# Two row tiles per step in the first attention pass of a six-layer transformer kernel, and one PSUM bank for its side work

## The chip, the cores and the metric

The kernel runs on one core of one Trainium2 chip. The metric is the device time of one execution in microseconds; the time of a kernel is the median of several executions. A core has five engines with instruction streams of their own: TensorE (PE; its weight loads are shown apart, as PEld), VectorE (DVE), ScalarE (ACT), GpSimd (POOL) and SyncE (SP), which here issues the DMAs. Each stream is executed in its order, and streams wait for each other by semaphores. PSUM has eight banks of 128 x 512 float32; matmuls write there, and DVE and ACT read there.

## The reference

x is 4 sequences of 512 tokens of 256 channels. After a layer norm, six layers run, each of self attention, cross attention and a GELU network, and at the end a mixture of 8 experts with top-2 routing:

```python
NL, D, H, DFF = (6, 256, 16, 1024)
HD = D // H
...
def _attn(q, k, v, mask):
    scores = jnp.einsum('bqhd,bkhd->bhqk', q, k) / np.float32(np.sqrt(HD))
    scores = jnp.where(mask[:, None, None, :], jnp.float32(-jnp.inf), scores)
    w = jax.nn.softmax(scores, axis=-1)
    return jnp.einsum('bhqk,bkhd->bqhd', w, v)
...
for i in range(NL):
    xn = _adaln(x, noise_emb, n1_w[i], n1_b[i])
    q, k, v = jnp.split(xn @ qkv_w[i].T, 3, axis=-1)
    ...
    x = x + _attn(q, k, v, src_mask).reshape(B, L, D) @ so_w[i].T
    xn = _adaln(x, noise_emb, n2_w[i], n2_b[i])
    ...
    x = x + _attn(q, k, v, ctx_mask).reshape(B, L, D) @ co_w[i].T
    xn = _adaln(x, noise_emb, n3_w[i], n3_b[i])
    h = jax.nn.gelu(xn @ f1_w[i].T + f1_b[i], approximate=False)
    x = x + (h @ f2_w[i].T + f2_b[i])
```

(The quoted lines are slightly joined; q and k are rotated by position, and in cross attention k and v come from the context.) A head has only 16 channels, so the attention is 16 heads x 512 x 512 scores per sequence and attention.

## The kernel before

**Jobs and slots.** One attention of one sequence is a job: 8 jobs in a layer (4 self, 4 cross), 48 in all. The work is pipelined in slots. In slot k the engines run the first pass of job k, the second pass of job k-1, the end of job k-2 (normalise, output projection, and behind a cross job its feed-forward network), and the head of job k+1 (norm, query and key projections, splitting). Slots whose end has a feed-forward network are called long here, the others short; four short and four long ones alternate in a layer.

**The two passes.** Queries and keys are split into three bfloat16 parts (high, mid, low), and a score is the sum of six part products. The parts are written to DRAM (`bounce`) and loaded again as a stack of 6 x 16 = 96 rows for each head, so that one bfloat16 matmul with 96 to 99 rows gives all six products. The first pass (L719) computes for each head and each tile of 128 queries the scores (128 x 512) into one of three PSUM banks (`ps1`), and DVE takes the negative row maximum (L933). The maxima are turned (chunk "M"), copied by ACT, and a DMA puts them as two more rows into the query stack. The second pass (L694) computes the scores transposed and shifted by the maximum, in two banks (`ps2`), and ACT takes the exponential (L762) into `prob`. A matmul may fill a `ps2` bank only when the exponential two before it is done (`s_prob`). After every four exponentials four matmuls of 32 columns each (L707, four heads on four column tiles; float32, so that each is two instructions in the trace) add prob times v into `psv`.

**A unit.** A slot has 16 units. A unit on PE is four times (one first-pass matmul, one second-pass matmul), with the four-head product "pv" after the second of them. The order is written out in `slot` of the tensor block.

**Side chunks.** All else on PE is cut into chunks of one PSUM bank and put at one of 32 places (two in each unit) by `CHUNK_PLACES`, `FFN1_PLACES`, `FFN2_PLACES` and `SHIFT_PLACES`. Two banks `side` are used in turn: a chunk waits (`begin`) only for the reader of the chunk two before it. The chunks: T1 (transpose the attention output), T2, O (output projection), HT and LT (transposes of a normed tile; LT for the feed-forward network), HQ, HK, HV (query, key and value projection), M, F1 (feed-forward, first layer, 8 chunks in two bundles of four) and F2 (second layer, two chunks). T1, HQ, HK, O and F2 are read by DVE; HT, LT, T2, HV, M and F1 by ACT. F1's reader is the GELU itself (L834), with a table load ahead and behind.

**The splitting chain.** DVE multiplies HQ and HK with cosine and sine, POOL adds the terms (L557, L558), ACT rounds to the high part (L802), POOL takes the rest (L560), ACT the mid part (L806), POOL the low part (L562). When the low part is there, SP issues one write of all three parts (768 KB, once for the queries and once for the keys), waits for both, and issues the loads of the stacks: 12 DMAs of 128 KB and the mask row for heads 0 to 7 (`load_stack(j, 0)`), then the two shift rows of the job before, then as much for heads 8 to 15. The first pass of a job can begin when the stacks of heads 0 to 7 are there.

## Time and profile before

| what | value |
| --- | --- |
| time before, median of 3 runs | 4818.79 us (4811.88 to 4828.0) |
| span of the profiled execution | 4811.2 us |
| first first-pass matmul / last pv | 113 us / 4240 us |
| short slot, long slot | 67 to 68 us, 103 to 106 us |
| PE, DVE, ACT, POOL busy | 93%, 60%, 55%, 15% |
| mean granted TensorE clock | 0.963 of full speed |

The attention and feed-forward layers take 4127 us of the span; ahead of them lie 113 us of preparation, behind them 571 us with the last network and the experts. A PE record of a pipelined matmul lasts from its start to its modelled end, which is longer than the distance to the next one; so what a matmul costs is read from the distance of starts in the timeline, not from its mean.

### The profile page before, as it was taken

The page shows a single profiled execution, that of the slowest core. Times are in us where ns is not written, and L with a number is a line of the kernel's source. Part 1 is how long each engine was busy: PE and PEld are TensorE (multiplying, and loading weights), DVE is VectorE, ACT ScalarE, POOL GpSimd, SP SyncE. Part 2 cuts the span into 40 slices and gives each one's busy share as a digit, 9 for nine tenths or more (in the row PEclk, how much of TensorE's full clock was granted, in tenths as well). Part 3 has the DMA queues.
Part 4 walks back from the last instruction along what each step waited for, and adds up shares of the span by engine and source line. Part 5 has one row for each costly group of instructions (what it writes and reads, how often), then busy time and mean ns, then how long its engine had stood idle before and what let it go on. Part 6 is the DMA issues. An engine that isn't in the chain of part 4 may idle for free. (4 is left out here: it accounts for less than half of the span.)

```text
span 4811.2 us, 74161 instructions
## 1 busy us (share of the span) xinstructions
PE 4472.5 (93%) x21558; PEld 2219.7 (46%) x21558; DVE 2875.6 (60%) x5847; ACT 2636.0 (55%) x4666; POOL 734.4 (15%) x434
## 2 busy tenths in 40 slices
PE   3899999999999999999999999999999999968999
PEld 1244455433544444455434555344554334455666
DVE  3777656577666577655677555776566776322111
ACT  1466655566555566555566555666555665621221
POOL 3221111112121121111112111211111121000000
PEclk7899999999999999999999999999999999988999
DMA  5444422344322434232444223343223442010000
GB/s 146 75 98 78 74 48 46 69 89 78 61 42 52 82 72 89 48 59 41 86 89 80 41 41 54 88 81 74 46 49 68 89 80 50 1 36 9 18 18 26
DMA packets 165264, 297.17 MB, mean 62 GB/s; under 512 B 26352, under 2 KB 131840, under 8 KB 146432
## 3 DMA queue, kind: packets, MB, share of 16 engines
q1 hardware_dynamic: 164864, 292.23, 31.5%
q8 instruction: 202, 3.31, 0.3%
q14 instruction: 198, 1.62, 0.1%
HBM read 212.18 MB, written 77.59 MB: 60 GB/s over the span
## 5 line engine op out<-in xcount | busy, mean ns | idle before, releaser
L933 DVE TENSOR_REDUCE negmax<-ps 128x1 f32<-128x512 f32 x3072 | 1981.1, 684 | 754.5 <-PE ps L719 734.6
L762 ACT ACTIVATE prob<-ps 128x512 f32<-128x512 f32 x3072 | 1718.0, 595 | 1148.7 <-PE ps L694 1115.2
L719 PE MATMUL ps<-kstack,qstack 97*128 97x512 bf16 x3072 | 1200.6, 392 | 105.6 <-DMA kstack<-maskrow 56.3
L694 PE MATMUL ps<-qstack,kstack 99*128 99x512 bf16 x3072 | 1192.9, 389 | 84.8 <-ACT prob L762 65.5
L707 PE MATMUL psv<-prob,v 128*32 128x512 f32 x6144 | 832.8, 614 | 0.7 <-ACT prob L762 0.7
L719 PEld LDWEIGHTS ps<-kstack,qstack 97*128 97x128 bf16 x3072 | 300.6, 98 | 997.3 <-DVE negmax L933 599.0
L694 PEld LDWEIGHTS ps<-qstack,kstack 99*128 99x128 bf16 x3072 | 301.8, 98 | 646.9 <-ACT prob L762 454.8
L557 POOL TENSOR_TENSOR rot<-ropep 128x512 f32<-128x512 f32 x96 | 122.0, 1270 | 2624.2 <-DVE ropep L965 2593.3
L971 DVE TENSOR_TENSOR x<-x,side 128x512 f32<-128x512 f32 x144 | 99.0, 688 | 475.3 <-PE side L614 475.3
L673 PE MATMUL side<-anat,wf 128*128 128x256 f32 x1536 | 343.6, 382 | 0.9 <-ACT anat L792 0.9
L614 PE MATMUL side<-wf,hT 128*128 128x256 f32 x1536 | 339.9, 379 | 1.9 <-issue 1.9
L614 PEld LDWEIGHTS side<-wf,hT 128*128 128x128 f32 x1536 | 292.0, 190 | 46.8 <-issue 2.7
L673 PEld LDWEIGHTS side<-anat,wf 128*128 128x128 f32 x1536 | 290.4, 191 | 45.0 <-issue 5.5
L1336 DVE SCALAR_TENSOR_TENSOR x<-eps,we,x 128x256 f32<-128x256 f32 x128 | 56.1, 480 | 389.1 <-PE eps L1201 389.1
L1238 ACT ACTIVATE hg<-eps,b 128x512 f32<-128x512 f32 x128 | 88.0, 687 | 363.5 <-PE eps L1189 363.5
L562 POOL TENSOR_TENSOR parts<-rot,parts 128x1024 bf16<-128x1024 f32 x96 | 204.1, 2126 | 324.0 <-ACT parts L806 324.0
L560 POOL TENSOR_TENSOR rot<-rot,parts 128x1024 f32<-128x1024 f32 x96 | 204.6, 2132 | 273.0 <-ACT parts L802 273.0
L707 PEld LDWEIGHTS psv<-prob,v 128*32 128x32 f32 x6144 | 121.5, 108 | 263.5 <-issue 188.8
L834 ACT ACTIVATE hT<-side,f1b 128x256 f32<-128x256 f32 x384 | 160.9, 470 | 131.2 <-PE side L673 130.6
L1189 PE MATMUL eps<-zT,w 128*128 128x512 f32 x512 | 227.8, 598 | 0.8 <-DVE x L1317 0.8
L1201 PE MATMUL eps<-w,hg 128*128 128x256 f32 x1024 | 226.4, 379 | 0.0
L1201 PEld LDWEIGHTS eps<-w,hg 128*128 128x128 f32 x1024 | 194.4, 190 | 40.5 <-issue 9.6
(140 smaller groups left out, 3789.6 us busy)
## 6 DMA issues: line engine op xcount, KB each, us to landing
bounce<-parts SPq DMA_DIRECT2D x96, 768.0 KB, 3.7
qstack<-bounce SPq DMA_DIRECT2D x576, 128.0 KB
kstack<-bounce SPq DMA_DIRECT2D x576, 128.0 KB
ctxT<-in_ctxT SPq DMA_DIRECT2D x24, 512.0 KB, 5.5
nw<-in_nwT SPq DMA_DIRECT2D x18, 512.0 KB, 11.3
w<-in_w SPq DMA_DIRECT2D x16, 512.0 KB, 4.4
wself<-in_wself SPq DMA_DIRECT2D x24, 256.0 KB, 5.1
wcross<-in_wcross SPq DMA_DIRECT2D x24, 256.0 KB, 4.2
```

The lines of the kernel that those rows point to most:

```text
L560: nc.gpsimd.tensor_tensor(rot[:, :, :], rot[:, :, :], parts[:, 0, :, :], ALU.subtract).then_inc(s_r1, 1)
L562: nc.gpsimd.tensor_tensor(parts[:, 2, :, :], rot[:, :, :], parts[:, 1, :, :], ALU.subtract).then_inc(s_low, 1)
L614: mm = nc.tensor.matmul(bank[:, i * D:(i + 1) * D], act_T[:, k, t * P:(t + 1) * P], w[:, k, :], start=(k == 0), stop=(k == nk - 1))
L673: mm = nc.tensor.matmul(bank[:, i * D:(i + 1) * D], wf1[:, kk, f * P:(f + 1) * P], nT[:, kk, th * (S // 2):(th + 1) * (S // 2)], start=(kk ...
L694: nc.tensor.matmul(ps2[:, slot_of(j, n, RING2), :], kk[:, h, kt * P:(kt + 1) * P], q[:, h, :], start=True, stop=True).then_inc(s_p2full, 1)
L707: mm = nc.tensor.matmul(psv[32 * i:32 * i + 32, 0, :], v[j % B][:, kt, (HD + 1) * h:(HD + 1) * h + 32], prob[:, 4 * (u % 2) + i, :], start ...
L719: nc.tensor.matmul(ps1[:, slot_of(j, n, RING1), :], q[0:SHIFT_ROW, h, t * P:(t + 1) * P], kk[0:SHIFT_ROW, h, :], start=True, stop=True).th ...
L762: nc.scalar.activation(prob[:, 4 * (u % 2) + i, :], ps2[:, slot_of(j, n, RING2), :], ACT.Exp, scale=HD ** -0.5).then_inc(s_prob, 1)
L834: ins = nc.scalar.activation(hT[:, f, :], bank[:, i * D:(i + 1) * D], ACT.Gelu, bias=f1b[:, f:f + 1])
L933: nc.vector.tensor_reduce(negmax[:, h // 8, t, h % 8:h % 8 + 1], ps1[:, slot_of(j, n, RING1), :], AX, ALU.max, negate=True).then_inc(s_p1f ...
L1189: mm = nc.tensor.matmul(ps[:, f, :], w1[:, i, k, f * P:(f + 1) * P], zT[:, k, c * S:(c + 1) * S], start=(k == 0), stop=(k == KD - 1))
L1201: mm = nc.tensor.matmul(ps[:, 4 + 2 * (n % 2) + m, q * D:(q + 1) * D], hg[:, n % 2, f, t * P:(t + 1) * P], w2[:, i, f, :], start=(f == 0), ...
```

## The change

- The heads are taken in pairs, one of heads 0 to 7 with one of heads 8 to 15. Of each stack, three part products (48 rows) and a mask row lie in one half of the 128 partitions, and the other three in the other half, the halves swapped for heads 8 to 15. The first pass uses only the first three products (high x high, high x mid, mid x high), 49 rows, so the two heads of a pair stand in rows 0 to 48 and 64 to 112, and their two matmuls go to two row tiles and two PSUM banks. One `tensor_reduce` then gives both heads' maxima (128 x 2 from 128 x 1024). The second pass uses all rows from 0 to 113.
- `ps1` has four banks (two pairs), and `side` one in place of two: each chunk now waits for the reader of the chunk before it. All places are set anew, with tables for short and for long slots.
- A unit on PE is now: two second-pass matmuls, a chunk, four first-pass matmuls (two pairs), pv, two second-pass matmuls, a chunk.
- F1 is read by DVE, which adds the bias, and one GELU over 2048 elements (in place) takes each half; the F1 chunks lie at eight places in a row, and F2 is cut into four chunks.
- Each part is written to DRAM as soon as it is there, once for each product it is part of (12 writes of 256 KB a job in place of 2 of 768 KB), and the loads are 4 of 192 KB and 2 mask rows for the first products and 4 of 192 KB for the second, for each half of the heads. The key split stands one unit later in short slots (places 18 and 20 in place of 16 and 18).

The core of the diff:

```diff
-RING1 = 3
 RING2 = 2
+PAIRS = 32
...
-CHUNK_PLACES = {
-    "HV": [1, 3], "T1": [4, 5, 6, 7], "HT": [5, 6], "HQ": [7, 8], "HK": [10, 11],
-    "T2": [11, 12], "O": [13, 14], "LT": [19, 20],
+SHORT_PLACES = {
+    "HV": [1, 3], "T1": [2, 4, 6, 7], "HT": [5, 8], "HQ": [9, 10], "HK": [12, 14],
+    "T2": [16, 17], "O": [18, 20],
 }
-SHIFT_PLACES = (20, 4)
-FFN1_PLACES = (22, 28)
-FFN2_PLACES = (25, 31)
+LONG_PLACES = {
+    "T1": [1, 3, 5, 7], "HV": [2, 4], "HT": [6, 8], "T2": [9, 10], "HQ": [11, 14], "O": [12, 13],
+    "HK": [15, 16], "LT": [18, 19], "F1": [20, 21, 22, 23, 24, 25, 26, 27], "F2": [28, 29, 30, 31],
+}
+SHIFT_PLACES = (19, 4)
...
-    "LT": dict(stats=[30, 31, 32, 33], aggregate=34, newton=35, tiles=[35, 35, 35, 35]),
+    "LT": dict(stats=[13, 13, 13, 13], aggregate=14, newton=16, tiles=[16, 16, 17, 17]),
...
-SPLIT_PLACES = (10, 12, 16, 18)
+SHORT_SPLIT = (13, 15, 18, 20)
+LONG_SPLIT = (17, 19, 22, 23)
+GELU_PLACES = (24, 28)
...
-        ps1 = psum("ps1", RING1)
+        ps1 = psum("ps1", 4)
-        side = psum("side", 2)
+        side = psum("side", 1)
...
-                sp.wait_ge(s_low, place.jobs(j, 2) + w + 1)
-                    sp.dma_start(bounce[w].rearrange("r (t p) n -> p (r t) n", p=P),
-                                 parts[:, :, :, :].rearrange("p r t n -> p (r t) n")).then_inc(s_bounce[w], 16)
+                sp.wait_ge((s_hi, s_mid, s_low)[part], place.jobs(j, 2) + w + 1)
+                for r in range(NPROD):
+                    if order[r] == part:
+                        src = low if part == 2 else parts[w][:, part, :, :]
+                        sp.dma_start(bounce[w][r].rearrange("(t p) n -> p t n", p=P), src[:, :, :]).then_inc(s_bounce[w], 16)
...
                 n = number[(k, what, c)]
-                if n >= 2:
-                    pe.wait_ge(s_read[n % 2], place.at(n // 2, CHUNKS_PER_LAYER // 2))
-                return side[:, n % 2, :]
+                if n >= 1:
+                    pe.wait_ge(s_read, place.at(n, CHUNKS_PER_LAYER))
+                return side[:, 0, :]
...
-                nc.tensor.matmul(ps1[:, slot_of(j, n, RING1), :], q[0:SHIFT_ROW, h, t * P:(t + 1) * P], kk[0:SHIFT_ROW, h, :],
-                                 start=True, stop=True).then_inc(s_p1full, 1)
+                for e in range(2):
+                    rows = slice(first_rows(e), first_rows(e) + FIRST_ROWS)
+                    mm = nc.tensor.matmul(ps1[:, 2 * (n % 2) + e, :], qs[j % 2][rows, 8 * e + m, t * P:(t + 1) * P],
+                                          ks[j % 2][rows, 8 * e + m, :], start=True, stop=True)
+                mm.then_inc(s_p1full, 1)
...
+                    if p2:
+                        pass2(k - 1, u, 0)
+                        pass2(k - 1, u, 1)
+                    for what, c in plan[2 * u]:
+                        side_work(k, what, c)
+                    if p1:
+                        pass1(k, 2 * u)
+                        pass1(k, 2 * u + 1)
+                    if u and p2:
+                        pv(k - 1, u - 1)
...
+                    if p2:
+                        pass2(k - 1, u, 2)
+                        pass2(k - 1, u, 3)
+                    for what, c in plan[2 * u + 1]:
+                        side_work(k, what, c)
...
+            def gelu(k, th):
+
+                wait_read(act, place, k, "F1", 4 * th + 3)
+                nc.scalar.activation(hT[th][:, :, :], hT[th][:, :, :], ACT.Gelu).then_inc(s_gelu, 1)
+                act.preload_act_table_set(EXP_SET)
...
+                nc.vector.tensor_reduce(out_at, ps1[:, 2 * (n % 2):2 * (n % 2) + 2, :], AX, ALU.max,
                                         negate=True).then_inc(s_p1free, 1)
...
+                elif what == "F1":
+                    th, cc = divmod(c, 4)
+                    for i in range(2):
+                        f = 2 * cc + i
+                        ins = nc.vector.tensor_scalar(hT[th][:, f, :], bank[:, i * D:(i + 1) * D], f1b[:, f:f + 1], None, ALU.add)
+                    ins.then_inc(s_read, 1)
```

How this stands on PE. First, a stretch without a side chunk before the change (L719 is the first pass, L694 the second, L707 is pv):

```order
L693 ISA
L694 MATMUL ps<-qstack,kstack 128x512 [waits probs_ready]
L718 ISA
L719 MATMUL ps<-kstack,qstack 128x512 [waits scores_reduced]
L693 ISA
L694 MATMUL ps<-qstack,kstack 128x512 [waits probs_ready]
L704 ISA
L707 MATMUL psv<-prob,v 32x512 [waits probs_ready]
L707 MATMUL psv<-prob,v 32x512 x3
```

The same stretch after the change (L771 is the first pass, L744 the second, L757 is pv), from the third second-pass matmul of a unit on:

```order
L743 ISA
L744 MATMUL ps<-qstack,kstack 128x512 [waits probs_ready]
L743 ISA
L744 MATMUL ps<-qstack,kstack 128x512 [waits probs_ready]
L768 ISA
L771 MATMUL ps<-kstack,qstack 128x512 [waits scores_reduced]
L771 MATMUL ps<-kstack,qstack 128x512
L768 ISA
L771 MATMUL ps<-kstack,qstack 128x512 [waits scores_reduced]
L771 MATMUL ps<-kstack,qstack 128x512
L754 ISA
L757 MATMUL psv<-prob,v 32x512 [waits probs_ready]
```

Where a first-pass matmul stood between any two of the second pass, four of the second pass now follow each other (two of one unit and two of the next, if no chunk is between), and the first-pass matmuls stand together ahead of pv.

The two query-projection chunks of a short slot on PE, before (chunk_read0 and chunk_read1 are the two banks):

```order
L606 MATMUL side<-xnT,wcross 128x512 [waits chunk_read0]
L606 MATMUL side<-xnT,wcross 128x512
L718 ISA
L719 MATMUL ps<-kstack,qstack 128x512 [waits scores_reduced]
L693 ISA
L694 MATMUL ps<-qstack,kstack 128x512 [waits probs_ready]
L718 ISA
L719 MATMUL ps<-kstack,qstack 128x512 [waits scores_reduced]
L693 ISA
L694 MATMUL ps<-qstack,kstack 128x512 [waits probs_ready]
L595 ISA
L606 MATMUL side<-xnT,wcross 128x512 [waits chunk_read1]
```

and after:

```order
L652 MATMUL side<-xnT,wcross 128x512 [waits chunk_read]
L652 MATMUL side<-xnT,wcross 128x512
L743 ISA
L744 MATMUL ps<-qstack,kstack 128x512 [waits probs_ready]
L743 ISA
L744 MATMUL ps<-qstack,kstack 128x512 [waits probs_ready]
L641 ISA
L652 MATMUL side<-xnT,wcross 128x512 [waits chunk_read]
```

Between a chunk at an odd place and one at the next even place only two matmuls are left, and the second chunk waits for the reader of the first.

## Rows read from the trace of the kernel before

**Rows 1.** The page's first part: busy us (share of the span) and instructions of each engine.

```profile
PE 4472.5 (93%) x21558; PEld 2219.7 (46%) x21558; DVE 2875.6 (60%) x5847; ACT 2636.0 (55%) x4666; POOL 734.4 (15%) x434
```

**Rows 2.** Groups by line: names, shapes, count | busy us, mean ns | idle before, releasers.

```profile
L933 DVE TENSOR_REDUCE negmax<-ps 128x1 f32<-128x512 f32 x3072 | 1981.1, 684 | 754.5 <-PE ps L719 734.6 <-issue 13.8
L762 ACT ACTIVATE prob<-ps 128x512 f32<-128x512 f32 x3072 | 1718.0, 595 | 1148.7 <-PE ps L694 1115.2 <-issue 8.6 <-PE psv L707 2.4
...
L834 ACT ACTIVATE hT<-side,f1b 128x256 f32<-128x256 f32 x384 | 160.9, 470 | 131.2 <-PE side L673 130.6
...
L802 ACT ACTIVATE parts<-rot 128x1024 bf16<-128x1024 f32 x96 | 101.0, 1052 | 50.2 <-POOL rot L558 37.4 <-DMA bounce<-parts 12.8
...
L952 DVE TENSOR_TENSOR anat<-side,recip 128x256 f32<-128x256 f32 x192 | 81.5, 424 | 6.6
```

**Rows 3.** Busy time of each engine in a short and a long slot, PEclk, DMA share, GB/s.

```profile
1067.40:1134.80 67.40, 66.17 (x345) 26.38 (x344) 53.24 (x105) 45.61 (x83) 13.52 (x8) 1.00 0.44 79
...
1409.83:1513.21 103.38, 97.14 (x481) 52.46 (x480) 62.00 (x124) 59.90 (x106) 15.84 (x9) 0.97 0.26 46
```

**Rows 4.** Timeline of PE, one unit without a chunk: start, us, what, count.

```profile
1118.56 1.06 PE L707 MATMUL psv<-prob,v 128*32 128x512 f32 x8
1119.56 0.39 PE L719 MATMUL ps<-kstack,qstack 97*128 97x512 bf16 x1
1119.79 0.38 PE L694 MATMUL ps<-qstack,kstack 99*128 99x512 bf16 x1
...
1120.86 0.39 PE L694 MATMUL ps<-qstack,kstack 99*128 99x512 bf16 x1
...
1121.35 0.39 PE L694 MATMUL ps<-qstack,kstack 99*128 99x512 bf16 x1
1121.67 0.64 PE L707 MATMUL psv<-prob,v 128*32 128x512 f32 x4
```

**Rows 5.** Timeline of ACT in the same unit: its four exponentials.

```profile
1120.21 2.25 ACT L762 ACTIVATE prob<-ps 128x512 f32<-128x512 f32 x4
```

**Rows 6.** Timeline of PE in slot 48, which has no first pass.

```profile
4181.58 1.06 PE L707 MATMUL psv<-prob,v 128*32 128x512 f32 x8
...
4184.46 1.06 PE L707 MATMUL psv<-prob,v 128*32 128x512 f32 x8
```

**Rows 7.** Timeline of PE in a long slot, ahead of the LT chunk.

```profile
1452.60 0.39 PE L719 MATMUL ps<-kstack,qstack 97*128 97x512 bf16 x1 [1.76 <-DVE negmax L933]
...
1454.13 0.61 PE L719 MATMUL ps<-kstack,qstack 97*128 97x512 bf16 x1
...
1457.69 1.11 PE L600 MATMUL side<-ident,xnat 128*128 128x128 f32 x4 [2.52 <-DVE xnat L925]
```

**Rows 8.** Timeline of PE: a T2 and a key-projection chunk, and what comes next.

```profile
1091.92 0.60 PE L600 MATMUL side<-ident,anat 128*128 128x128 f32 x4
1092.36 1.88 PE L606 MATMUL side<-ctxT,wcross 128*128 128x512 f32 x4
1094.07 0.38 PE L719 MATMUL ps<-kstack,qstack 97*128 97x512 bf16 x1
```

**Rows 9.** Timeline of DVE: the reader of that key-projection chunk.

```profile
1094.28 0.69 DVE L964 TENSOR_TENSOR ropep<-side,sin 128x512 f32<-128x512 f32 x1 [1.55 <-PE side L606]
1094.88 0.68 DVE L965 TENSOR_TENSOR ropep<-side,cos 128x512 f32<-128x512 f32 x1
1095.48 0.68 DVE L933 TENSOR_REDUCE negmax<-ps 128x1 f32<-128x512 f32 x1
```

**Rows 10.** Timeline of PE: one F2 chunk (two row tiles of x).

```profile
1477.54 7.07 PE L614 MATMUL side<-wf,hT 128*128 128x256 f32 x32
1484.44 0.38 PE L719 MATMUL ps<-kstack,qstack 97*128 97x512 bf16 x1
```

**Rows 11.** Timeline of POOL: the key's low part.

```profile
1110.20 2.12 POOL L562 TENSOR_TENSOR parts<-rot,parts 128x1024 bf16<-128x1024 f32 x1 [1.43 <-ACT parts L806]
```

**Rows 12.** The stretch in which the stacks of heads 0 to 7 are loaded (columns as in 3).

```profile
1116.13:1130.13 14.00, 13.64 (x72) 3.66 (x68) 10.91 (x19) 9.93 (x20) 0.00 (x0) 1.00 0.84 115
```

**Rows 13.** Timeline of PE: the first first-pass matmul of the next slot.

```profile
1130.46 0.39 PE L719 MATMUL ps<-kstack,qstack 97*128 97x512 bf16 x1 [0.55 <-DMA kstack<-maskrow]
```

More of the change, by code:

```diff
@@ L360, in slot_chunks @@
             tail, head = k >= 2, k + 1 < 2 * NJ
-            ffn = tail and is_cross(k - 2)
+            places = LONG_PLACES if is_ffn(k) else SHORT_PLACES
             plan = {i: [] for i in range(2 * SLOT_UNITS)}
@@ L677, in side_work @@
                 elif what == "F2":
-                    wait_read(pe, place, k, "F1", 4 * c + 2)
-                    wait_read(pe, place, k, "F1", 4 * c + 3)
-                    project(begin(k, what, c), wf2, hT, 0, FT)
+                    th, t = divmod(c, 2)
+                    if t == 0:
+                        pe.wait_ge(s_gelu, place.at(2 * cross_before(k - 2) + th + 1, 2 * B))
+                    bank = begin(k, what, c)
+                    for f in range(FT):
+                        mm = nc.tensor.matmul(bank[:, 0:D], hT[th][:, f, t * P:(t + 1) * P], wf2[:, f, :], start=(f == 0), stop=(f == FT - 1))
+                    mm.then_inc(s_full, 1)
             def pass2(j, u, i):
@@ L781, in modulate @@
                 wait_filled(act, place, k, what, c)
-                bank, read = bank_of(k, what, c)
                 row, b = norm_row(k, what)
@@ new lines, in slot @@
+                ffn = is_ffn(k)
+                splits = LONG_SPLIT if ffn else SHORT_SPLIT
+                for at in range(2 * SLOT_UNITS):
+                    u, half = divmod(at, 2)
+                    if p2:
+                        exp(k - 1, u, 2 * half)
+                        exp(k - 1, u, 2 * half + 1)
+                    for what, c in plan[at]:
+                        side_work(k, what, c)
+                    if head and at == GUESS_PLACES["HT"]:
+                        rstd_guess(k, "HT")
+                    if ffn and at == GUESS_PLACES["LT"]:
+                        rstd_guess(k, "LT")
+                    if head and at in splits:
+                        step, n = divmod(splits.index(at), 2)[::-1]
+                        (hi, mid)[step](k + 1, n)
+                    if ffn and at in GELU_PLACES:
+                        gelu(k, GELU_PLACES.index(at))
+                    if half == 0:
+                        if u == 0 and tail:
+                            copy_group(k, k - 2, TT - 1)
+                        elif u and p2 and u % TT == 0:
+                            copy_group(k, k - 1, u // TT - 1)
@@ L968, in side_work @@
                     t0 = TT * (j % B) + 2 * c
-                    if what == "F2" and c == 0:
-                        dve.wait_ge(s_bias, place.at(cross_before(j) + 1, B))
                     nc.vector.tensor_tensor(x[:, t0:t0 + 2, :], x[:, t0:t0 + 2, :], bank.rearrange("p (t d) -> p t d", t=2),
-                                            ALU.add).then_inc(read, 1)
+                                            ALU.add).then_inc(s_read, 1)
             def head0():
@@ new lines, in slot @@
+                ffn = is_ffn(k)
+                for at in range(2 * SLOT_UNITS):
+                    u, half = divmod(at, 2)
+                    if half == 1 and p1:
+                        maximum(k, 2 * u)
+                        maximum(k, 2 * u + 1)
+                        if u == 8:
+                            shift_parts(k, 0)
+                    for what, c in plan[at]:
+                        side_work(k, what, c)
+                    for what, wanted in (("HT", head), ("LT", ffn)):
+                        places = NORM_PLACES[what]
+                        if not wanted:
+                            continue
+                        for t in range(TT):
+                            if at == places["stats"][t]:
+                                stats(k, what, t)
+                        if at == places["aggregate"]:
+                            aggregate(what)
+                        if at == places["newton"]:
+                            normalise(k, what)
+                        for t in range(TT):
+                            if at == places["tiles"][t]:
+                                normed(k, what, t)
@@ L1364 @@
     qkv = w("qkv_w")
+    inner = np.concatenate([head_of(g, i) * HD + np.arange(HD) for g in range(H // 4) for i in range(4)])
     cos, sin = rope_tables()
```

348 lines of the change are left out of this document (153 added, 195 removed).

## The prediction

> **What bounds the kernel now.** I began with the busy shares: TensorE is busy 93% of the span, VectorE 60%, ScalarE 55% [rows 1]. A busy record says nothing of what is gained if it gets shorter, so I read a short and a long slot [rows 3]: 67.4 us and 103.4 us, with PE covered for 66.2 and 97.1 us, DVE for 53 and 62, ACT for 46 and 60. PE, with its in-order waits, sets the slot. Then I took a unit apart in the timeline. pv holds PE for 1.00 us (1118.56 to 1119.56), and the unit repeats after 3.11 us [rows 4]. Eight 512-column bfloat16 matmuls stand in it at 0.22 us each (1119.56, 1119.79) = 1.76 us, and pv begins 0.32 us after the last of them, 0.10 more than a plain step. So a unit in which nothing waits costs 1.76 + 0.10 + 1.00 = 2.86 us, and 0.25 us of the 3.11 is a wait: the second-pass matmul at 1120.86 comes 1.07 us after the one at 1119.79, because its bank is freed only by an exponential that starts 0.42 us after its matmul (1120.21) and takes 2.25 / 4 = 0.56 us [rows 4, 5]. I call that the exponential ring. It is nearly covered today, since a first-pass matmul lies between any two of the second pass.
>
> Where chunks lie in a unit, they add their own time and cover the ring: 0.44 us for a transposing chunk, 1.71 us for a projection [rows 8], 6.90 us for an F2 chunk [rows 10], a quarter of that (1.72) for F1, which has as many instructions in four chunks. The chunks of a short slot sum to 8 x 0.44 + 8 x 1.72 + 2 x 0.33 = 18.0 us (the M chunk's 0.33 is an estimate, three quarters of a transposing chunk), those of a long one to 18.0 + 2 x 0.44 + 8 x 1.72 + 2 x 6.90 = 46.5 us. Check: short 16 x 2.86 + 18.0 = 63.8 of 67.4 us; long 92.3 of 103.4. The rest of a short slot is the ring. In a long slot some 7 us are the hole ahead of LT: PE idles 1.76 and 2.52 us, and from 1454.13 on the matmul records last 0.61 in place of 0.39 us, the lower of the two clock levels [rows 7].
>
> **The first pass.** Four steps of 0.22 = 0.88 us in a unit become two pairs. If two row tiles run at once, as pv's four column tiles do (eight instructions of 512 float32 columns in 1.00 us, where four on the full array take 1.71 [rows 4, 8]), a pair takes 0.22 us: 0.44. No row shows row tiles; the other end is 0.88. But the unit now changes its tiling three times (full, two row tiles, column tiles, full) and not twice. Around pv the trace has 0.10 us going in; for coming out, 1.00 us less the 0.85 that half of 1.71 gives is 0.15. I charge 0.10 for the new change, between 0 and 0.15. So a unit without waits costs 4 x 0.22 + 0.44 + 0.10 + 0.10 + 1.00 = 2.52 us, 0.34 less than 2.86. That gain is 16 x 0.34 = 5.4 us a slot. The Trainium skill, TensorEngine Tiling (Array Packing), Key Properties, says that a change of tiling mode drains TensorE; the 0.10 us ahead of pv agrees, and it speaks against a kernel that mixes three modes in each unit. The Trainium skill, TensorE: Matmul & The Clock Gate, Part 3 (Packing small matmuls), says that matmuls of different row tiles start some 4 ns apart; no trace here shows it, and by it the pair would be 0.22 us, the value already taken.
>
> **The ring loses its cover.** In a unit with no chunk at its odd place, four second-pass matmuls now follow each other: the first at 1.00 after pv, the third 1.07 later, the fourth when the second exponential ends, 0.42 + 2 x 0.56 + 0.07 = 1.6 after the first, so at 2.6. Then 0.32 to the first pair (a tiling change), 0.22, 0.32 to pv: 3.46 us. I take 3.42, that is 0.90 over 2.52. A row close to it: in slot 48, with no first pass at all, such a unit still takes 2.88 us [rows 6]; add 0.54 for the pairs and it is 3.42. So a bare unit gets slower by 0.31, though its PE work falls. By the new places a short slot has 9 such units (6 bare, 3 with a chunk at the even place only), a long one 1. A short chunk (0.44) at the odd place covers half: 0.46 is left, 4 times in a short slot.
>
> **One bank.** A chunk's reader starts 0.21 us after the next matmul could (1094.07, 1094.28) and, for a rope chunk, runs 1.20 us to the next DVE start, release with its tail 1.4 [rows 8, 9]. From an odd place to the next even one only two steps (0.44 us) lie between. Waits: after a query or key chunk 0.21 + 1.4 - 0.44 = 1.2 us; after a copy on ACT (0.6 us, [rows 2]) 0.4; after O (0.69) 0.5; after F1 on DVE (two of 0.42 by the 256-element row, [rows 2]) 0.7; a chunk put right behind another at one place pays all, about 0.9. The other way, even to odd, pairs, pv and two steps (2.0 us) cover every reader. In a short slot seven such neighbours and one double place sum to 0.4 + 0.4 + 0.9 + 0.6 + 0.2 + 1.2 + 0.4 + 0.4 = 4.5 us. Short slot: 16 x 2.52 + 18.0 + 9 x 0.90 + 4 x 0.46 + 4.5 = 72.7 us, **5.3 more** than 67.4.
>
> A long slot has 15 neighbours of this kind. T1 to its next, 4 times, 0.66 with the ring: 2.6. Double places 4 and 19: 0.9 and 2.0 (M waits behind two exponentials, then LT's reader). T2 0.9, HQ to O 1.2, O to HQ 0.5. Four after F1: 2.8. F2 0.2. At 15 the key chunk's reader also waits for POOL's rope of the query (two POOL adds) and for two maxima: 2.1. LT at 18: the DVE must do the key chunk, the Newton steps, four tiles and two pairs of maxima after 16, so I keep 2.8 of hole and 2 us of low clock, against some 7 now. The GELU: ACT does 1052 ns for 1024 elements and 595 for 512 [rows 2], so 2048 take about 2.0 us, plus two table loads, in one block at 24 and at 28; 0.7 shows. Long slot: 40.3 + 46.5 + 0.9 + 2.6 + 2.9 + 2.6 + 2.8 + 0.2 + 2.1 + 4.8 + 0.7 = 106.4 us. The mean long slot is 104.5 (four lie between 103 and 106), so **1.9 more**. Not on the path: 16 GELUs of 0.47 us [rows 2] become two, and maxima, where 684 ns for 512 elements and 424 for 256 make about 1.2 us for 1024 in place of 2 x 0.62; DVE needs 2.4 us of a 2.5 us unit at most, so it is a close second but not the bound.
>
> **The loads.** In a short slot the key's low part ends at 1112.3 [rows 11], the loads of 1.5 MB run from 1116.1 to about 1130.1 at a DMA share of 0.84 [rows 12], and the next slot's first matmul waits 0.55 us for them [rows 13]: this chain is late already. After the change it starts a unit later, but 5.5 units of 3.42 us follow, less 3.3 for mid and low: 15.5 us are left. The first pass needs half of the bytes: write 2.5 and load 7 us, in time. The shift rows of the job before, which the second pass needs at once, stand behind both halves: 2.5 + 14 + 0.7 = 17.2 us, late by 1 to 2. SP's own issue falls from 13 DMAs to 10. Twelve writes a job move 73.7 MB more, of 297 now; they go out while the loads don't run. I charge 0.5 us a short slot, between 0 and 4.
>
> **Sum.** 24 short slots x 5.8 + 24 long x 1.9 = 185 us. The last two slots have no first pass to cover anything: slot 49 has eight F1 chunks each behind a reader (8 x 1.1) and an exposed GELU and table load (3.3), some 15 us in all; the first slot, set by DVE, saves 3. In all 185 + 12 = 197: 4811 + 197 = 5008 us. The median of the runs lies 8 us over the profiled span; I forecast 5010 us.
>
> **Rivals.** (a) **Faster: the freed PE time is kept.** The tiling changes cost nothing (768 units x 0.10 = 77 us), the LT hole closes in all long slots because its norm is spread over four places (4.8 x 24 = 115), and half of the bank waits of long slots vanish because DVE issues half as many maxima (4.4 x 24 = 105): 5008 - 297 = 4711 us. It decides where a reader is released within 0.44 us of its chunk. For it: PE is covered 93%. Against: a single exponential takes 0.56 us and a rope read 1.2, more than 0.44 whatever DVE has before it. Chance 0.12. (b) **Row tiles don't run at once**: each pair takes 0.44 us, 768 x 0.44 = 338 us more, 5346 us. For it: no row shows them. Against: column tiles do run so. 0.07. (c) **The shift rows bind**: 4 us for each short slot in place of 0.5: 24 x 3.5 = 84, 5092 us; for it the 0.55 us wait at share 0.84 and above. 0.11. (d) **Gain and loss cancel**, at half of the ring and bank costs and with free tiling changes: about 4811 us. 0.05. Forecast: 0.65.
>
> **How the numbers follow.** A change of 0.3% (14 us) is about what a measurement of this kernel can tell from none. Faster 0.13, within 0.04, slower 0.83. The range goes from 4810 (leaving out rival (a)) to 5130 (over (c), leaving out (b)).
>
> **What would show it.** In the profile after, short slots of 72 to 74 us and long ones of 105 to 108; bare units of 3.4 us; second-pass starts 1.07 us apart at the third of four; the two matmuls of a pair starting within 0.05 us (if 0.2, rival (b)); waits of side matmuls for DVE and ACT readers of 0.4 to 1.2 us between odd and even places, some 80 to 150 us of them in 24 + 24 slots for each kind of reader; a first second-pass matmul of a slot that waits for the shift rows. The forecast is wrong if bare units fall under 3.1 us, or if long slots fall under 100.

## The result, and the profile after

The changed kernel takes 5116.3 us (median of 4 runs, 5109.4 to 5123.8) beside 4822.1 us for the kernel before on the same chip (4811.9 to 4828.0): 1.060 times as long, interval 1.058 to 1.063. The profiled execution has a span of 5115.7 us at a mean granted clock of 0.959. The forecast was 5010 us with a range from 4810 to 5130: the sign and the range hold the result, but of 304.5 us that the span grew by, the sum had only 197. The result lies 14 us under the upper end of the range.

The busy shares of the engines:

```profile
PE 4382.7 (86%) x21558; PEld 2008.9 (39%) x21558; DVE 2950.8 (58%) x4741; ACT 2530.7 (49%) x4330; POOL 762.7 (15%) x446
```

TensorE works less than in [rows 1], 4383 us for 4473, and is busy for 86% of the span in place of 93%. So the added time is waiting. A short and a long slot, each from the reader of its first T2 chunk to that of the next slot's, and all slots from the first value chunk of slot 1 to that of slot 47, after (columns as in [rows 3]):

```profile
1098.23:1172.13 73.90, 64.40 (x348) 21.98 (x344) 52.62 (x74) 44.83 (x83) 13.51 (x9) 1.00 0.37 94
...
1412.98:1522.09 109.11, 94.34 (x481) 47.05 (x480) 64.94 (x110) 56.22 (x93) 15.82 (x9) 0.98 0.25 59
...
178.81:4358.13 4179.32, 3630.70 (x18648) 1547.35 (x18648) 2676.98 (x4117) 2302.19 (x3982) 670.18 (x389) 0.98 0.32 80
```

and the last of these stretches before:

```profile
178.14:4069.26 3891.12, 3715.84 (x18641) 1752.31 (x18640) 2629.86 (x5216) 2396.18 (x4274) 670.72 (x389) 0.98 0.36 67
```

In the stretch of the slots 288.2 us were added (4179.3 less 3891.1), 0.7 us ahead of it and 15.6 us behind it. The forecast had 185 + 12. The short slot shown takes 73.9 us (forecast 72.7, and 0.5 for the loads), a long one, so measured, 109.1 to 112.3 (forecast 106.4). Over all slots, counted from value chunk to value chunk, the 24 short ones grew from 68.1 to 75.0 us in the mean and the 21 long ones from 104.5 to 110.1; about 0.5 us of the short ones' growth is a shift of that mark, which stands one place later in long slots. So the larger part of what the sum lacks lies in the long slots.

A unit without a chunk on TensorE, to be held against [rows 4]:

```profile
1196.96 1.06 PE L757 MATMUL psv<-prob,v 128*32 128x512 f32 x8
1197.95 0.61 PE L744 MATMUL ps<-qstack,kstack 114*128 114x512 bf16 x2
1199.04 0.88 PE L744 MATMUL ps<-qstack,kstack 114*128 114x512 bf16 x2 [0.47 <-ACT prob L818]
1199.84 0.61 PE L771 MATMUL ps<-kstack,qstack 49*128 49x512 bf16 x4
1200.38 1.07 PE L757 MATMUL psv<-prob,v 128*32 128x512 f32 x8
```

From pv to pv it is 3.42 us, to the digit what the ring was forecast to make of it, where it was 3.11. The third second-pass matmul starts 1.09 us behind the first (1197.95, 1199.04) after 0.47 us of waiting for an exponential; the row of ACT has the same 2.25 us for four as in [rows 5], now with 1.18 us of idle time ahead of it:

```profile
1194.96 2.25 ACT L818 ACTIVATE prob<-ps 128x512 f32<-128x512 f32 x4 [1.18 <-PE ps L744]
```

All four first-pass matmuls with the change of tiling behind them take 0.54 us (1199.84 to 1200.38): 2 x 0.22 + 0.10. Two row tiles do run at once: the records of a pair start within 0.01 us of each other, and the next pair 0.22 us later.

Now the single bank. In the long slot two query, two output and two key chunks follow each other; four of the six, and what stands around them:

```profile
1416.22 1.88 PE L652 MATMUL side<-xnT,wself 128*128 128x512 f32 x4
1417.94 0.60 PE L744 MATMUL ps<-qstack,kstack 114*128 114x512 bf16 x2
1419.58 2.00 PE L660 MATMUL side<-wcross,hT 128*128 128x256 f32 x8 [1.04 <-DVE ropep L1013]
1421.50 0.61 PE L771 MATMUL ps<-kstack,qstack 49*128 49x512 bf16 x4
...
1425.21 0.60 PE L744 MATMUL ps<-qstack,kstack 114*128 114x512 bf16 x2
1426.15 1.98 PE L652 MATMUL side<-xnT,wself 128*128 128x512 f32 x4 [0.35 <-DVE x L1029]
...
1431.77 0.60 PE L744 MATMUL ps<-qstack,kstack 114*128 114x512 bf16 x2
1434.51 1.98 PE L652 MATMUL side<-xnT,wself 128*128 128x512 f32 x4 [2.15 <-DVE ropep L1013]
```

The bracket holds the idle time and who ended it. A chunk at an even place waits for the reader of the chunk at the odd place before it: 1.04 us, 0.35, and 2.15 for the key chunk. A bracket begins only at the modelled end of the matmul before, and so comes out short. From start to start, less two steps (0.44 us), the waits are 1.20 us (1417.94 to 1419.58; forecast 1.2), 0.50 (1425.21 to 1426.15; 0.5) and 2.30 (1431.77 to 1434.51; 2.1).

Then look at how far the next row stands from each chunk. The one that did not wait takes 1.72 us (1416.22 to 1417.94), as in [rows 8]; each that waited takes 1.92 (1419.58 to 1421.50, and the same for the other two). Of these 0.20 us, 0.10 is the change of tiling, which is in the sum once for each unit: the chunks that waited stand ahead of the row tiles, the other ahead of a second-pass matmul. A chunk that stands ahead of the row tiles and did not wait takes 1.81:

```profile
1165.49 1.88 PE L652 MATMUL side<-ctxT,wcross 128*128 128x512 f32 x4
1167.30 0.61 PE L771 MATMUL ps<-kstack,qstack 49*128 49x512 bf16 x4
```

Only the other 0.10 us was in no term. It goes with the weight load: for the chunk that did not wait, the load begins 0.22 us ahead of its matmul (1416.00, 1416.22), for one that waited at the same moment. This is read from the records; no run separates it.

```profile
1434.51 0.30 PEld L652 LDWEIGHTS side<-xnT,wself 128*128 128x128 f32 x2 [2.64 <-DVE ropep L1013]
```

Then the hole ahead of LT, the answer to [rows 7], and on VectorE and GpSimd what stands before it:

```profile
1439.24 0.88 PE L744 MATMUL ps<-qstack,kstack 114*128 114x512 bf16 x2 [0.67 <-ACT prob L818]
1444.06 1.11 PE L646 MATMUL side<-ident,hT 128*128 128x128 f32 x4 [3.94 <-DVE hT L970]
1445.10 1.04 PE L771 MATMUL ps<-kstack,qstack 49*128 49x512 bf16 x4
1446.07 1.75 PE L757 MATMUL psv<-prob,v 128*32 128x512 f32 x8
1447.76 0.60 PE L744 MATMUL ps<-qstack,kstack 114*128 114x512 bf16 x2
```

```profile
1438.32 0.73 DVE L970 TENSOR_SCALAR hT<-x,mv,y 128x256 f32<-128x256 f32 x2
1438.97 2.35 DVE L980 TENSOR_REDUCE negmax<-ps 128x2 f32<-128x1024 f32 x2
1441.24 1.61 DVE L987 CAST mpart<-negmax 128x32 bf16<-128x32 f32 x1
...
1443.20 0.73 DVE L970 TENSOR_SCALAR hT<-x,mv,y 128x256 f32<-128x256 f32 x2
```

```profile
1440.69 2.12 POOL L602 TENSOR_TENSOR rot<-rot,parts 128x1024 f32<-128x1024 f32 x1 [8.48 <-ACT parts L853]
```

TensorE waits 3.94 us for the last of four normed tiles. Two were normed at 1438.3, the last two only at 1443.2; between them stand two pairs of maxima and the shift parts, whose first cast took 1.61 us while GpSimd's addition ran, and ended within 0.05 us of it (1442.85, 1442.81). Behind the hole the matmuls run at the lower clock for one chunk, two pairs and a pv: 3.70 us to 1447.76, where at full clock 0.44 + 0.54 + 1.00 would stand. In other long slots the lower clock lasts longer. The slot before this one has the same hole and the same work up to the pv behind the first F1 chunk, and takes 13.28 us for it (1331.80 to 1345.08) in place of 10.13 (1444.06 to 1454.19), with a granted clock of 0.50 from 1332 to 1344:

```profile
1331.80 1.11 PE L646 MATMUL side<-ident,hT 128*128 128x128 f32 x4 [3.94 <-DVE hT L970]
...
1345.08 1.06 PE L757 MATMUL psv<-prob,v 128*32 128x512 f32 x8
...
1454.19 1.07 PE L757 MATMUL psv<-prob,v 128*32 128x512 f32 x8
```

### The profile page after: what moved, and what is told of

Same layout as the page of the kernel before. It is cut to its first block and busy times, and to the rows that moved or that the text cites. A ratio compares the mean times of both kernels' runs of the same rounds, so it can differ in the third digit from the quotient of the medians.

```text
span 5115.7 us, 70957 instructions
## 1 busy us (share of the span) xinstructions
PE 4382.7 (86%) x21558; PEld 2008.9 (39%) x21558; DVE 2950.8 (58%) x4741; ACT 2530.7 (49%) x4330; POOL 762.7 (15%) x446
## 5 line engine op out<-in xcount | busy, mean ns | idle before, releaser
L818 ACT ACTIVATE prob<-ps 128x512 f32<-128x512 f32 x3072 | 1666.8, 597 | 1459.6 <-PE ps L744 1438.2
L980 DVE TENSOR_REDUCE negmax<-ps 128x2 f32<-128x1024 f32 x1536 | 1804.7, 1217 | 402.5 <-PE ps L771 402.5
L744 PE MATMUL ps<-qstack,kstack 114*128 114x512 bf16 x3072 | 1021.0, 388 | 211.1 <-ACT prob L818 154.2
L757 PE MATMUL psv<-prob,v 128*32 128x512 f32 x6144 | 841.4, 620 | 0.0
L744 PEld LDWEIGHTS ps<-qstack,kstack 114*128 114x128 bf16 x3072 | 236.2, 97 | 1267.4 <-ACT prob L818 711.7
L771 PE MATMUL ps<-kstack,qstack 49*128 49x512 bf16 x3072 | 487.5, 395 | 42.3 <-DMA kstack<-maskrow 21.2
L719 PE MATMUL side<-anat,wf 128*128 128x256 f32 x1536 | 388.2, 397 | 49.4 <-DVE hT L1018 31.4
L1018 DVE TENSOR_SCALAR hT<-side,f1b 128x256 f32<-128x256 f32 x384 | 168.1, 479 | 388.6 <-PE side L719 388.6
L719 PEld LDWEIGHTS side<-anat,wf 128*128 128x128 f32 x1536 | 294.0, 197 | 137.2 <-DVE hT L1018 57.6
L608 POOL TENSOR_TENSOR low<-rot,parts 128x1024 bf16<-128x1024 f32 x96 | 204.6, 2131 | 417.1 <-ACT parts L857 417.1
L757 PEld LDWEIGHTS psv<-prob,v 128*32 128x32 f32 x6144 | 122.4, 109 | 335.2 <-issue 219.5
L652 PE MATMUL side<-xnT,wself 128*128 128x512 f32 x384 | 196.8, 637 | 53.9 <-DVE ropep L1013 47.7
L646 PE MATMUL side<-ident,hT 128*128 128x128 f32 x576 | 106.5, 314 | 146.2 <-DVE hT L970 116.6
## 6 DMA issues: line engine op xcount, KB each, us to landing
nw<-in_nwT SPq DMA_DIRECT2D x18, 512.0 KB, 11.3
```

The lines of the kernel that those rows point to most:

```text
L608: nc.gpsimd.tensor_tensor(low[:, :, :], rot[:, :, :], parts[w][:, 1, :, :], ALU.subtract).then_inc(s_low, 1)
L652: mm = nc.tensor.matmul(bank, w[:, k, m * P:(m + 1) * P], act_T[:, k, :], start=(k == 0), stop=(k == KD - 1))
L719: mm = nc.tensor.matmul(bank[:, i * D:(i + 1) * D], wf1[:, kk, f * P:(f + 1) * P], nT[:, kk, th * (S // 2):(th + 1) * (S // 2)], start=(kk ...
L744: nc.tensor.matmul(ps2[:, n % RING2, :], kk[0:ROWS, h, kt * P:(kt + 1) * P], q[0:ROWS, h, :], start=True, stop=True).then_inc(s_p2full, 1)
L757: mm = nc.tensor.matmul(psv[32 * i:32 * i + 32, 0, :], v[j % 2][:, kt, (HD + 1) * h:(HD + 1) * h + 32], prob[:, 4 * (u % 2) + i, :], start ...
L771: mm = nc.tensor.matmul(ps1[:, 2 * (n % 2) + e, :], qs[j % 2][rows, 8 * e + m, t * P:(t + 1) * P], ks[j % 2][rows, 8 * e + m, :], start=Tr ...
```

## The experiments

All ratios are to the kernel before, timed on the same chip (median 4824.0 us for the first four kernels below, 4819.2 for the last three). Lines in the diffs are against the changed kernel unless said.

**Full array for the first pass.** Do the two row tiles save time, and how much?

```diff
-                    rows = slice(first_rows(e), first_rows(e) + FIRST_ROWS)
-                    mm = nc.tensor.matmul(ps1[:, 2 * (n % 2) + e, :], qs[j % 2][rows, 8 * e + m, t * P:(t + 1) * P],
-                                          ks[j % 2][rows, 8 * e + m, :], start=True, stop=True)
+                    rows = slice(0, HALF + BLOCK)
+                    mm = nc.tensor.matmul(ps1[:, 2 * (n % 2) + e, :], qs[j % 2][rows, m, t * P:(t + 1) * P],
+                                          ks[j % 2][rows, m, :], start=True, stop=True)
```

(The run besides scales the exponential down, and lets the first pass wait for all loads of its heads, of which only the wait at the start shows: 25.5 us for 21.2.)

> One edit to the changed kernel: the first pass uses 112 rows of the array for each matmul, so that the two of a pair lie on the same rows and can't run at once; order, banks, maxima and loads stay (the maxima are those of other heads and the exponential is scaled down, so the output isn't the reference's; the work is the same). Theory A (row tiles run at once and a change of tiling costs 0.10 us): a unit gets 0.44 - 0.10 = 0.34 us longer, 261 us in all: about 5380 us, and a pair of matmuls takes 0.44 us. Rival C (row tiling gained nothing net, since the drains eat it): 5116 us, within 20.

Measured: 5360.9 us (5354.3 to 5366.9), ratio 1.111 [1.109, 1.113]. The block of first-pass matmuls in a bare unit:

```profile
1092.38 0.88 PE L744 MATMUL ps<-qstack,kstack 114*128 114x512 bf16 x2 [0.67 <-ACT prob L819]
1093.09 1.03 PE L772 MATMUL ps<-kstack,qstack 112*128 112x512 bf16 x4
1094.05 1.06 PE L757 MATMUL psv<-prob,v 128*32 128x512 f32 x8
```

0.96 us (1093.09 to 1094.05), against 0.54 with row tiles. And the block begins 0.71 us after the second-pass matmul that waited, where with row tiles it is 0.80 to 0.81 (1199.04 to 1199.84): the change from the full array to row tiles costs 0.10 us, as charged. The same 0.10 shows behind chunks. With the full array a chunk ahead of the first pass takes 1.72 us if it did not wait (1221.68 to 1223.40), and 1.82 if it did:

```profile
1210.59 1.98 PE L652 MATMUL side<-xnT,wcross 128*128 128x512 f32 x4 [1.04 <-DVE ropep L1014]
1212.41 1.03 PE L772 MATMUL ps<-kstack,qstack 112*128 112x512 bf16 x4
```

With row tiles it is 1.81 and 1.92. So a wait makes a projection chunk 0.10 us longer, whatever the tiling behind it.

The time grows by 244.6 us over the changed kernel (261 expected). The rule of the Trainium skill, TensorEngine Tiling (Array Packing), Key Properties, that a change of mode drains TensorE, agrees with this 0.10 us. Rival (b), that row tiles do not run at once, is excluded.

**The second pair behind the odd chunk.** The ring loses its cover because the pairs stand together. Here one pair is put back between the second-pass matmuls:

```diff
                     if p1:
                         pass1(k, 2 * u)
-                        pass1(k, 2 * u + 1)
...
                     for what, c in plan[2 * u + 1]:
                         side_work(k, what, c)
+                    if p1:
+                        pass1(k, 2 * u + 1)
```

(On VectorE the second maximum moves behind the odd place's reader in the same way.)

> One edit to the changed kernel: the second pair of first-pass matmuls of each unit (and its maximum on DVE) stands behind the chunk of the odd place, between the second-pass matmuls of one unit and those of the next, in place of beside the first pair ahead of pv. It puts cover (a pair and two tiling changes, 0.42 us) into the gap where the exponential ring and the one side bank wait, and adds two changes of tiling to each unit. Theory A (ring and bank waits are what the change cost): a bare unit falls from 3.42 to about 3.13 us, each wait after a reader gets 0.4 us shorter, short slots fall by 3 to 4 us and long ones by 2 to 4: 4930 to 4980 us. Rival B (the changes of tiling are what cost): 768 units x 0.20 us more = 5270 us.

Measured: 5010.6 us (5003.1 to 5017.5), ratio 1.039 [1.036, 1.041], 105.7 us less than the changed kernel. A bare unit:

```profile
1099.11 1.06 PE L757 MATMUL psv<-prob,v 128*32 128x512 f32 x8
...
1100.65 0.39 PE L771 MATMUL ps<-kstack,qstack 49*128 49x512 bf16 x2
1101.19 0.88 PE L744 MATMUL ps<-qstack,kstack 114*128 114x512 bf16 x2 [0.15 <-ACT prob L819]
...
1102.32 1.07 PE L757 MATMUL psv<-prob,v 128*32 128x512 f32 x8
```

3.21 us in place of 3.42, with 0.15 us of waiting for an exponential in place of 0.47. The expected 3.13 was short by what is left of the wait. The rival's 5270 is excluded: the ring is what the pair covers. The run lies outside theory A's range too (4930 to 4980), with a gain of 106 us where 136 to 186 were expected. Five changes of tiling stand in the unit now, where the changed kernel has three, but A had counted them; 0.08 us of a bare unit is what its row shows, and the rest of the miss stays open. A short slot fell only from 73.9 to some 72 us, a long one to 105 to 108.

**All LT tiles at place 16.**

```diff
-    "LT": dict(stats=[13, 13, 13, 13], aggregate=14, newton=16, tiles=[16, 16, 17, 17]),
+    "LT": dict(stats=[13, 13, 13, 13], aggregate=14, newton=16, tiles=[16, 16, 16, 16]),
```

> One edit to the changed kernel: the four normed tiles for LT are all made at place 16, ahead of two pairs of maxima and the shift parts, in place of two at 16 and two at 17. Theory A (the hole ahead of LT is a queue on DVE): PE's wait for the normed tiles falls from 3.9 us to under 1 us in each long slot, and the stretch at the lower clock behind it goes with it: 24 x 4 to 5 us less, 4990 to 5020 us. Rival D (the hole is set by the late key chunk and the rope, and the clock stays low there anyway): less than 30 us change, 5090 to 5116 us.

Measured: 5010.5 us (5008.3 to 5013.4), ratio 1.038 [1.036, 1.040], 105.8 us less than the changed kernel, at a clock of 0.973 for 0.959. VectorE norms four tiles in a row, 1.38 us in all, and goes on to the maxima then.

TensorE's waits for normed tiles (us in all, times, longest), in the changed kernel and here:

```profile
PE side L646 <- DVE hT L970: 116.6, 24, 19.3
```

```profile
PE side L646 <- DVE hT L970: 36.0, 3, 19.3
```

The three that are left (19.3, 11.3 and 5.4 us) stand at the start and in the tail, in both kernels. The 21 that are gone are the holes of the long slots, 3.84 us each in the mean, 80.6 us in all. The stretch behind the hole, from the LT chunk to the pv behind the first F1 chunk, falls from 11.2 to 10.1 us in the mean of these slots: another 22 us, nearly all of the rest. It still takes 9.0 to 11.5 us, so the lower clock is not gone from it. That is theory A's size (4990 to 5020); the rival's 5090 to 5116 is excluded.

**Three banks for the first pass, two for the chunks, and the pair between.** The banks are split as before the change; maxima are then taken one by one, since a pair of neighbouring banks no longer exists.

```diff
-        ps1 = psum("ps1", 4)
+        ps1 = psum("ps1", 3)
...
-        side = psum("side", 1)
+        side = psum("side", 2)
...
-                nc.vector.tensor_reduce(out_at, ps1[:, 2 * (n % 2):2 * (n % 2) + 2, :], AX, ALU.max,
-                                        negate=True).then_inc(s_p1free, 1)
+                for e in range(2):
+                    nn = 2 * n + e
+                    at = 4 * e + m % 4
+                    dve.wait_ge(s_p1full, place.jobs(j, 64) + nn + 1)
+                    nc.vector.tensor_reduce(negmax[:, m // 4, t, at:at + 1], ps1[:, slot_of(j, nn), :], AX, ALU.max,
+                                            negate=True).then_inc(s_p1free, 1)
```

(and the order of the experiment with the pair between)

> The edit of e1_pair_between, and besides two side banks again: the first pass has a ring of three single banks (one maximum for each matmul, as before the change), and each chunk waits for the reader of the chunk two before it. Theory A (one bank costs about a quarter of a microsecond to one and a half at each odd to even neighbour): against e1_pair_between what is left of the bank waits and of the exposed weight loads goes, 2 to 3 us in short slots and 5 to 7 us in long ones, 170 to 240 us less: 4720 to 4800 us. Rival E (the readers' own work binds, so that a second bank frees nothing, and single maxima make DVE slower by 0.17 us a unit): no less than e1_pair_between, up to 130 us more.

Measured: 4772.2 us (4770.0 to 4774.6), ratio 0.989 [0.987, 0.991]. So 238.4 us less than with the order alone, and 1.1% faster than the kernel before. Single maxima instead of joint ones and a ring of three go with the second bank; no run separates them, so the 238 us are what the bank gives less whatever they cost. That is inside A's 4720 to 4800 and far from the rival's 5010 and more, though the gain was to be 170 to 240 us and lies at its upper end. The LT hole is still there (2.92 us in one long slot), which leads to the next step.

**The same with all LT tiles at place 16.** The LT edit above on top.

> e5_order_banks with the LT tiles all made at place 16 as in e3_lt_tiles. In e5_order_banks PE still idles 1.3 and 2.9 us ahead of LT in a long slot, and runs a stretch at the lower clock. Theory A (the gain of e3_lt_tiles, 105 us, is a thing of its own and adds): 24 x 3 to 4.5 us less than e5_order_banks: 4665 to 4700 us, faster than the kernel before by some 3%. Rival D (with the banks gone another wait takes the place): 4740 to 4772 us.

Measured: 4694.0 us (4693.5 to 4695.0), ratio 0.976 [0.974, 0.978]: 78.2 us less than without it, and the best version here. Its short and its long slot:

```profile
1048.90:1117.14 68.24, 65.25 (x346) 23.58 (x344) 54.33 (x105) 44.91 (x82) 13.53 (x8) 1.00 0.42 102
1382.48:1480.58 98.10, 94.08 (x482) 48.87 (x480) 65.76 (x142) 56.10 (x92) 15.83 (x9) 0.98 0.28 66
```

The short slot is still 0.8 us longer than in [rows 3], the long one 5.3 us shorter, and TensorE is back at 93% busy. A bare unit takes 3.21 us as in the experiment with the pair between, 0.10 more than before the change. Over all slots the short ones are 1.8 us longer than before the change (69.9 us in the mean for 68.1) and the long ones 7.2 shorter (97.3 for 104.5). What the version gains, it gains in the long slots.

**The banks alone, the changed order kept.** Is the pair between needed at all?

> One edit to the changed kernel, with its order kept: two side banks, and a ring of three single first-pass banks with a maximum for each matmul. The bank waits and exposed weight loads go (I count 5.9 us in short and 11 us in long slots, 405 us), but the fourth first-pass matmul of a unit, 0.2 us behind the third, needs the maximum of the first, which is there only 1.1 us after the first starts: 0.7 us a unit, 540 us. Theory A: 5200 to 5300 us, with PE waiting for DVE's maxima for some 500 us. Rival F (the maxima are quick enough, the one bank was all that mattered): 4720 to 4850 us, without the new order being needed.

Measured: 5786.3 us (5770.5 to 5796.3), ratio 1.202 [1.199, 1.206], at a clock of 0.928. Three banks don't hold two pairs: the fourth first-pass matmul waits for a maximum, 732 us in all. Two bare units, first one at the full clock, then one of those that follow:

```profile
1193.55 1.07 PE L768 MATMUL psv<-prob,v 128*32 128x512 f32 x8
...
1195.62 0.88 PE L755 MATMUL ps<-qstack,kstack 114*128 114x512 bf16 x2 [0.47 <-ACT prob L828]
...
1197.61 0.39 PE L782 MATMUL ps<-kstack,qstack 49*128 49x512 bf16 x1 [0.57 <-DVE negmax L992]
1197.92 1.41 PE L768 MATMUL psv<-prob,v 128*32 128x512 f32 x8
...
1209.64 1.93 PE L768 MATMUL psv<-prob,v 128*32 128x512 f32 x8
...
1212.81 1.10 PE L755 MATMUL ps<-qstack,kstack 114*128 114x512 bf16 x2 [0.26 <-ACT prob L828]
...
1215.23 0.61 PE L782 MATMUL ps<-kstack,qstack 49*128 49x512 bf16 x1 [0.36 <-DVE negmax L992]
1215.77 1.93 PE L768 MATMUL psv<-prob,v 128*32 128x512 f32 x8
```

4.37 us (1193.55 to 1197.92), then 6.13 (1209.64 to 1215.77): the granted clock fell from 1.00 to 0.50, the lower of the two levels, and stayed there with 0.6 us of waiting in a unit. The rival's 4720 to 4850 is excluded. The mechanism that theory A named is there, but A had 5200 to 5300, and the loss over the changed kernel, 670 us, is several times what it allowed. It counted 540 us of waits for maxima, where 732 were measured, and no loss of clock, where the mean fell from 0.959 to 0.928. How the rest of the miss divides, no run shows. The four banks of the first pass belong to the new order: with four, and one left for the chunks, the chunks pay; with three, the pairs do. Of the orders run here, the one with a pair between gets on with three.

**The kernel before, with its LT norm one step earlier.** The gain of the LT places, tried without the change (lines of the kernel before):

```diff
-    "LT": dict(stats=[30, 31, 32, 33], aggregate=34, newton=35, tiles=[35, 35, 35, 35]),
+    "LT": dict(stats=[29, 30, 31, 32], aggregate=32, newton=34, tiles=[34, 34, 34, 34]),
...
-GUESS_PLACES = {"HT": 2, "LT": 18}
+GUESS_PLACES = {"HT": 2, "LT": 16}
```

> The kernel before with one edit: the norm steps for LT stand one step earlier each (statistics at steps 29 to 32, aggregate 32, Newton and the four tiles at 34, guess at place 16). Theory A (the hole ahead of LT, some 7 us of each long slot before, is a queue of DVE steps, and each step earlier gives back its time): 1 to 3 us for each long slot, 4750 to 4800 us. Rival D (it is set by DVE steps that run slowly beside GpSimd's long additions, wherever they stand): within 15 us of 4820.

Measured: 4791.4 us (4773.9 to 4809.9 in 10 runs), ratio 0.994 [0.993, 0.997]. So about 28 us of the best version's 125 are to be had without the change; the other 97 are the change's, with order and banks mended. This is no exact parting, since the LT places of both kernels differ. It is within A's 4750 to 4800, and the runs spread over 36 us. TensorE's waits for normed tiles fell by 48 us (70.7 to 22.8), so more was taken away than was gained; its waits for exponentials rose by 45 (65.5 to 110.5). What rival D names does occur: in one slot a step of the norm on VectorE lasted as long as GpSimd's operation beside it.

```profile
1450.78 2.12 POOL L560 TENSOR_TENSOR rot<-rot,parts 128x1024 f32<-128x1024 f32 x1 [6.76 <-ACT parts L802]
1450.81 2.11 DVE L918 SCALAR_TENSOR_TENSOR lnv<-y 128x4 f32<-128x4 f32 x1
```

## Why the forecast was right, and where it was short

**The pairs: right.** A pair takes 0.22 us, both with their change of tiling 0.54. The run with the full array prices them at 245 us, so the work that the change means to save is saved.

**The ring: right in the bare unit.** 3.42 us was forecast and measured. Putting one pair back between gave back 106 us, of the ring and of the bank waits together.

**The bank waits: right.** Counted from start to start, the waits at even places are 1.20 us (forecast 1.2), 0.50 (0.5) and 2.30 (2.1); after F1 it is 0.69 (0.7). Of M's two, the first is 1.0 (0.9) and the second, for which the LT chunk waits, 1.3 (2.0). The GELU shows 0.34 (0.7). GELU and joint maximum last 1.9 and 1.2 us (estimated 2.0 and 1.2; mean ns in the middle):

```profile
L980 DVE TENSOR_REDUCE negmax<-ps 128x2 f32<-128x1024 f32 x1536 | 1804.7, 1217 | 402.5 <-PE ps L771 402.5
```

**Mis-sized: a chunk behind a wait costs more than the wait.** The sum added waits to chunks of 1.72 and 0.44 us. A projection behind a wait takes 0.10 us more than that and its change of tiling, and one right behind a second-pass matmul that itself waited up to 0.10 more; a transposing chunk takes 0.05 more. Added up over the chunks of the two slots shown, this is 0.5 us in the short and 1.1 in the long one, 24 x 1.6 = 39 us in all if they stand for the rest. In the sum the error was to take a chunk's price from a place where it had no wait ahead of it [rows 8].

**Mis-sized: the LT hole and the clock behind it.** 2.8 us and 2 us of low clock were charged, 4.8 in all. The hole is 3.84 us in the mean by its brackets, 4.0 from start to start. Behind it the long slot shown loses (1.04 - 0.59) + (0.97 - 0.54) + (1.69 - 1.00) = 1.6 us to the lower clock (0.59 us is a transposing chunk behind a wait and ahead of the row tiles at full clock), and others up to 3.2 more; in the mean it is 2.6. That makes 6.6 us, or 1.8 more than charged, 38 us in the 21 long slots that have the hole. What was said to stand ahead of LT (tiles, two pairs of maxima) does; the shift parts, and a cast that waits for GpSimd, had been left out.

**Mis-sized the other way.** 12 us were charged for the shift rows' loads; all waits of second-pass matmuls for them come to 5.6 us, and that is one wait:

```profile
L744 PE MATMUL ps<-qstack,kstack 114*128 114x512 bf16 x3072 | 1021.0, 388 | 211.1 <-ACT prob L818 154.2 <-DMA qstack<-mrow 5.6 <-issue 0.8
```

The kernel now moves 372 MB for 297, and no slot waits for it: rival (c) is excluded. The two terms, 4 us more at the ends and these 6 us less make 75 us of the 108 that the sum lacks. Some 30 us stay open; by the short slot shown, which is 0.7 us longer than forecast even with its chunks' excess counted, part of them is in the ring.

**What was luck.** The upper end of the range, 5130 us, stood over rival (c), and (c) did not come true; the result came within 14 us of it by terms that no rival had. The long slots, at 109 to 112 us, are over the 105 to 108 that were named as a sign, and the wait for the shift rows, another sign, is missing. The 8 us between profiled span and median were no property of the kernel: the profiled run had been the fastest, and now the two differ by 0.6 us.

**Rival (a), faster: its premises fell.** It asked that changes of tiling cost nothing, that the LT hole close and that half of the bank waits of long slots vanish. None of it holds in this kernel. The last two made by hand, with a pair between, give 4694 us where (a) had said 4711; that the numbers are close is chance, since that kernel also pays five changes of tiling in a unit and has the ring half covered. The new first pass is worth its 0.34 us a unit only where nothing else is taken for it.

**The parts of the result,** by experiments, from the changed kernel down: one pair between 106 us, a second side bank 238 us, LT tiles together 78 us (106 when done alone). The effects overlap: the LT edit was worth 106 us with the one bank and 78 with two.

## What to carry to other kernels

When an instruction gets shorter, ask what it was covering: here 0.34 us saved in a unit left 0.90 us of a ring of two banks uncovered, where it had been 0.25, and placing a piece of the shortened work in the gap bought back more than a third of the loss. Where one PSUM bank does the work of two, every use can wait, and each wait costs its length and some 0.1 us more. Price a step from a place where it has the same thing ahead of it as it will have.

## What the runs showed of the hardware

- **A float32 chunk behind a wait takes longer.** 1.92 us for a projection chunk in place of 1.81 where the tiling changes behind it, 1.82 in place of 1.72 where it does not; 0.49 for a transposing one of 0.44. Its weight load begins together with its first matmul, not 0.22 us ahead. I had expected only the wait to count.
- **A short VectorE step can last as long as GpSimd's operation beside it.** The cast of 128x32 took 1.61 us in place of 0.18 (L989 in the same chain) and ended with an addition on GpSimd of 2.12 us; in the last experiment a step of 128x4 took 2.11 us, where most of its kind take 0.15, and ended within 0.02 us of an addition of 2.12 us. The Trainium skill, SBUF — State Buffer, section SBUF: two separate sides, has a port pair that VectorE and GpSimd share as an exclusive lock; the cast's end within 0.05 us of the addition's agrees with a lock, and so do the 0.02 us; no run here took GpSimd's work away to prove it.
- **The clock fell where TensorE waited somewhat more.** With 0.47 us of waiting in a unit of 3.42 us the granted clock stayed at 1.00 for whole slots; after units of 4.37 us with 0.47 and 0.57 it fell to 0.50, and the bare units then took 6.13 us. So a wait can cost a multiple of itself.
- **A change of tiling from the full array to row tiles costs 0.10 us,** and two row tiles of 49 rows and 512 columns take no longer (0.22 us) than one such matmul on the full array.
